# Two graph layers on one core: the steps behind each chunk move from VectorE to GpSimd, Exp to ScalarE, the first loads of adj to SyncE

## The reference, cut to what matters

```python
h = jnp.maximum(_layernorm(x, axis=-1), 0.0)          # x (4096, 128)
# layer 1, in the ball model; adj (4096, 4096)
h = proj(mobius_matvec(weight, h)); h = proj(mobius_add(h, hyp_bias)); x_tangent = logmap0(h)
support_t = adj @ x_tangent
h = proj(expmap0(support_t)); xt = relu(logmap0(h)); x = x + proj(expmap0(xt))
# layer 2: attention over the edges of adj
h = jnp.maximum(_layernorm(x, axis=-1), 0.0)
in_fts = context @ W_common.T                          # context (4096, 256)
logits = (in_fts @ w_left + b_left)[:, None] + (in_fts @ w_right + b_right)[None, :]
logits = where(logits >= 0, logits, 0.2 * logits); logits = where(adj <= 0, -inf, logits)
x = x + relu(softmax(logits, axis=-1) @ h)
```

## Time and profile before

| what | us |
|---|---|
| median of 3 runs | 655.37 (650.78 to 664.92) |
| the profiled execution | 653.83 |
| its span in the trace | 652.0 |
| busy DVE, PE, ACT, POOL | 543.6, 509.1, 422.5, 227.4 |

### The profile page before, as it was taken

One profiled execution on the slowest core, in us unless ns is written; L12 is line 12 of the kernel. 1 busy time (PEld: TensorE's weight loads), 2 busy tenths in 40 slices (PEclk: granted clock), 3 DMA queues, 4 the chain that ended last, 5 costly groups with the idle time before them and its releaser, 6 DMA issues.

```text
span 652.0 us, 9315 instructions
## 1 busy us (share of the span) xinstructions
PE 509.1 (78%) x2695; PEld 318.2 (49%) x2695; DVE 543.6 (83%) x1057; ACT 422.5 (65%) x553; POOL 227.4 (35%) x217
## 2 busy tenths in 40 slices
PE   0360899758768948899898575779898989999995
PEld 0350343223223313344242254568787878787874
DVE  3488797959779836697777899999999999999995
ACT  0584785535345533567474987488888897989881
POOL 4370017984966706910101567420202020202110
PEclk9995799979969968899999888799999999999999
DMA  8991599969969999999999101001110101011010
GB/s 198 273 191 32 106 244 284 259 150 231 237 120 245 142 198 268 238 252 296 252 288 249 35 2 32 14 21 35 24 41 18 33 16 32 16 32 32 0 32 16
DMA packets 164235, 84.51 MB, mean 130 GB/s; under 512 B 7248, under 2 KB 163152, under 8 KB 164208
## 3 DMA queue, kind: packets, MB, share of 16 engines
q1 hardware_dynamic: 93760, 49.30, 35.2%
q10 hardware_dynamic: 70192, 34.74, 25.9%
q0 software_dynamic: 256, 0.15, 0.1%
HBM read 79.96 MB, written 4.21 MB: 129 GB/s over the span
## 4 chain that ended last, share of the span: by engine, by line
DVE 41%; PE 15%; issue 13%; POOL 11%; DMA 10%; SPq 4%; ACTq 3%; ACT 2%; DVEq 1%; POOLq 0%
PE ps L620 11%; DMA room<-in_adj_dram 8%; DVE room L1091 6%; DVE room L1137 5%; DVE mask L1091 5%; POOL mask L458 4%; DVE room L1147 4%; DVE mask L1137 3%; PE ps L646 3%; DVE room L905 3%; POOL mask L453 3%; DVE mask L1147 3%; SPq L331 2%; DMA out_dram<-xk 2%; ACTq L664 2%
## 5 line engine op out<-in xcount | busy, mean ns | idle before, releaser
L620 PE MATMUL ps<-room 128*128 128x512 f32 x512 | 248.7, 636 | 66.7 <-DVE room L905 45.8
L772 ACT ACTIVATE mask<-room 128x1024 int8<-128x1024 f32 x128 | 134.8, 1054 | 124.1 <-DVE room L905 111.3
L905 DVE STREAM_TRANSPOSE room<-room 128x512 f32<-128x512 f32 x256 | 171.4, 694 | 48.3 <-DMA room<-in_adj_dram 16.9
L620 PEld LDWEIGHTS ps<-room 128*128 128x128 f32 x512 | 98.1, 201 | 211.8 <-DVE room L905 109.9
L646 PE MATMUL ps<-room 128*128 128x258 f16 x1152 | 141.8, 285 | 28.5 <-DVE room L1147 28.5
L646 PEld LDWEIGHTS ps<-room 128*128 128x128 bf16 x1152 | 115.2, 101 | 53.9 <-DVE room L1147 34.3
L646 PE MATMUL ps<-room,mask 128*128 128x258 f16 x896 | 101.2, 273 | 9.5 <-DVE h_room L1161 6.4
L646 PEld LDWEIGHTS ps<-room,mask 128*128 128x128 bf16 x896 | 86.3, 97 | 23.1 <-DVE h_room L1161 8.1
L818 ACT ACTIVATE room<-mask 128x2048 bf16 (+1 forms) x36 | 68.5, 1903 | 14.1 <-PE ps L646 14.0
L555 POOL TENSOR_TENSOR h_room<-h_room 128x512 f32<-128x512 f32 x7 | 9.9, 1408 | 146.5 <-DVE post L1172 146.5
L818 ACT ACTIVATE mask<-mask 128x2048 bf16 (+1 forms) x28 | 53.3, 1903 | 4.7 <-PE ps L646 4.7
(11 more groups left out here) (164 smaller groups left out, 551.5 us busy)
## 6 DMA issues: line engine op xcount, KB each, us to landing
room<-in_adj_dram SPq DMA_DIRECT2D x128, 256.0 KB, 8.9
room<-in_adj_dram ACTq DMA_DIRECT2D x128, 256.0 KB, 8.3
mask<-in_L_gnn_context_dram SPq DMA_DIRECT2D x16, 256.0 KB, 11.2
xk<-in_x_dram SPq DMA_DIRECT2D x32, 64.0 KB, 6.4
out_dram<-xk SPq DMA_DIRECT2D x32, 64.0 KB, 5.8
h_room<-out_dram SPq DMA_DIRECT2D x32, 64.0 KB, 2.5
out_dram<-h_room SPq DMA_DIRECT2D x28, 64.0 KB, 1.8
mask<-in_x_dram SPq DMA_DIRECT2D x8, 128.0 KB, 6.6
```

The source lines that it names most:

```text
L620: pe.matmul(acc[parity], xt[:, k, :], turned[:, k % TSLOTS, :], start=(k == 0), stop=(k == NK - 1)).then_inc(block_multiplied, 1)
L772: nc.scalar.activation(mc[:, half * HB:(half + 1) * HB, :], turned[:, slots:slots + HB, :], ACT.Sign).then_inc(half_signed, 1)
L905: v.transpose(turned[:, k % TSLOTS, :].rearrange("p (l b i) -> p b l i", l=L, b=NQ), loaded[:, g % XSLOTS, :, l * Q:(l + 1) * Q].rearrange ...
```

## The change

Of the post work, VectorE keeps relu, the two sums, statistics and variance. GpSimd takes shrink, the coefficient and the residual (now two steps over 128 by 512 elements: relu_u times coefficient, and that plus xk), and affine. What was one piece of the list (a product and its sums) is now two, and one piece stands behind each of shrink, residual and affine. Statistics and variance stand behind steps 28 to 30 instead of 23 to 25. The largest right value is a maximum on VectorE over r_col, a store of 128 elements to DRAM, a load of them into all partitions and a second maximum; both transfers are issued by GpSimd. The four factors are one Exp on ScalarE in chunk 7; GpSimd scales two of them. ScalarE's tanh moves to half 9 and normed of chunk p to half 2 of the chunk after the next. SyncE stores x1 behind tile 4 and loads x behind tile 6. SyncE issues all four quarters of the first four tiles of adj; ScalarE issues the first part of x ahead of weight and bias. Some scratch tiles (the left and right values, the products) get other places, and the loops over the chunks of phase 1 are written out on VectorE and GpSimd.

```diff
...
+                    first_tiles = isinstance(c, int) and c == 0 and g < XSLOTS
+                    for b in (0, 2, 1, 3) if first_tiles else LOW:
                         sp.dma_start(loaded[b * Q:(b + 1) * Q, g % XSLOTS], rows[g, b]).then_inc(
                             adj_in[g % XSLOTS], 16)
                     if isinstance(c, int) and c == 0 and g == XSLOTS - 1:
                         load_nodes(cx, cx_l, cx_in, range(NQ))
-                    if g == 1 and not (isinstance(c, int) and c < 2):
+                    if g == 4 and not (isinstance(c, int) and c < 2):
                         store_x1(c - 2)
-                    if g == 3 and not (isinstance(c, int) and c < 1):
+                    if g == 6 and not (isinstance(c, int) and c < 1):
...
+            def store_largest():
+                pool.wait_ge(top_ready, 1)
+                pool.dma_start(top_dram, extreme[:, 0:1]).then_inc(top_stored, 16)
+            def everyones_largest():
+                pool.wait_ge(top_stored, 16)
+                pool.dma_start(top_row, top_dram.rearrange("p a -> a p").broadcast_to([P, P])).then_inc(top_loaded, 16)
             def exponents():
-                R = extreme[:, 2:3].broadcast_to([P, NK])
+                pool.wait_ge(top_ready, 2)
+                R = extreme[:, 1:2].broadcast_to([P, NK])
                 pool.wait_ge(nl_stored, 16)
...
+                tt(a_col, a_col, lr[:, 0, :], ALU.subtract).then_inc(exponents_ready, 1)
+                tt(b_col, b_col, lr[:, 0, :], ALU.subtract).then_inc(exponents_ready, 1)
+            def scaled_weights():
+                pool.wait_ge(exponentials_done, 1)
+                two = factors[:, 2:4, :].rearrange("p a k -> p (a k)")
+                tt(two, two, constants[:, 1:2].broadcast_to([P, 2 * NK]), ALU.mult).then_inc(factors_ready, 1)
+            part_order = [last_part] + list(range(last_part))
+            turns = [(w, part) for part in part_order for w in range(2)]
+            def beside(n):
+                w, part = turns[n // 2] if n < 2 * len(turns) else (None, None)
+                if part is not None:
+                    product_of(w, part) if n % 2 == 0 else sum_of(w, part)
+                elif n == 2 * len(turns):
+                    sums_and_rows()
+                elif n == 2 * len(turns) + 1:
+                    store_largest()
+                elif n == 2 * len(turns) + 2:
+                    everyones_largest()
+                elif n == 2 * len(turns) + 3:
+                    exponents()
+            def shrink(p):
+                UI, RN, F, VN = (post[:, a:a + L] for a in (8, 12, 20, 24))
+                pool.wait_ge(sums_ready, p + 1)
+                chain = Steps(pool, post_step, p * POOL_POST)
+                chain(tt(post[:, 8:16], post[:, 0:8], powers[:], ALU.pow))
+                chain(nc.gpsimd.tensor_scalar(F, UI, ARTANH_RIM, 1.0, ALU.mult, ALU.min))
+                tt(VN, F, RN, ALU.mult).then_inc(shrunk_ready, 1)
+                chain(tt(post[:, 16:20], post[:, 4:8], powers[:, 0:L], ALU.pow))
+            def residual(p):
+                INV, TH_, TF, CO = (post[:, a:a + L] for a in (16, 28, 32, 56))
+                pool.wait_ge(tanh_ready, p + 1)
+                chain = Steps(pool, post_step, p * POOL_POST + 3)
+                chain(nc.gpsimd.tensor_scalar(TF, TH_, MAX_NORM, None, ALU.min))
+                chain(tt(CO, TF, INV, ALU.mult))
+                chain(tt(relu_u[:], relu_u[:], CO.unsqueeze(2).broadcast_to([P, L, D]), ALU.mult))
+                pool.wait_ge(xk_loaded, p * (16 * NQ) + 16 * NQ)
+                tt(xk[:], relu_u[:], xk[:], ALU.add).then_inc(x1_ready, 1)
+            def affine(p):
+                pool.wait_ge(var_ready, p + 1)
+                chain = Steps(pool, post_step, p * POOL_POST + 6)
+                nc.gpsimd.tensor_scalar(post[:, 44:48], mv[:, :, 0], -1.0, None, ALU.mult)
+                chain(tt(post[:, 48:52], post[:, 40:44], powers[:, 0:L], ALU.pow))
+                tt(post[:, 36:40], post[:, 44:48], post[:, 48:52], ALU.mult).then_inc(norm2_ready, 1)
+            POOL_POST = 7
...
+            beside(0)
+            beside(1)
+            for p in range(NC - 1):
+                shrink(p)
+                beside(3 * p + 2)
+                if p == NC - 2:
+                    scaled_weights()
+                residual(p)
+                beside(3 * p + 3)
+                affine(p)
+                beside(3 * p + 4)
...
-                    norms(NC - 1)
+                    shrink(NC - 1)
+                if g == 2:
+                    residual(NC - 1)
                 if g == 4:
-                    inverse_std(NC - 1)
+                    affine(NC - 1)
...
+            def load_x_high(l):
+                for b in HIGH:
+                    act.dma_start(by_l(x_in, l)[b * Q:(b + 1) * Q], x_l[l, b]).then_inc(x_in_sem[l], 16)
+            load_x_high(0)
             act.dma_start(W_in, weight).then_inc(weights_in, 16)
             act.dma_start(b_colv, bias.rearrange("(d a) -> d a", a=1)).then_inc(weights_in, 16)
             act.dma_start(bias_b, bias.rearrange("(a d) -> a d", a=1).broadcast_to([P, D])).then_inc(weights_in, 16)
                 for b in HIGH:
                     act.dma_start(loaded[b * Q:(b + 1) * Q, g % XSLOTS], rows[g, b]).then_inc(adj_in[g % XSLOTS], 16)
-            for l in range(L):
-                for b in HIGH:
-                    act.dma_start(by_l(x_in, l)[b * Q:(b + 1) * Q], x_l[l, b]).then_inc(x_in_sem[l], 16)
-            for g in range(XSLOTS):
-                load_high(adj_n[0], g)
+            for l in range(1, L):
+                load_x_high(l)
...
-                return {0: copy, 4: squares, 8: tanh, 15: normed}
+                return copy, squares, tanh, normed
             acc_of = [None]
             def signs(c, parity):
                 number = isinstance(c, int)
                 acc_of[0] = acc[1 - parity]
-                steps = {} if number and c == 0 else post_steps(c - 1)
+                steps = {}
+                if c >= 1:
+                    copy, squares, tanh, _ = post_steps(c - 1)
+                    steps = {0: copy, 4: squares, 9: tanh}
+                if c >= 2:
+                    steps[2] = post_steps(c - 2)[3]
+                if c == NC - 1:
+                    steps[7] = exponentials
...
+            def exponentials():
+                act.wait_ge(exponents_ready, 2)
+                every = factors[:].rearrange("p a k -> p (a k)")
+                nc.scalar.activation(every, every, ACT.Exp).then_inc(exponentials_done, 1)
             for c in range(NC):
                 signs(c, c % 2)
             acc_of[0] = acc[1]
-            last = post_steps(NC - 1)
-            last[0]()
+            last_copy, last_squares, last_tanh, last_normed = post_steps(NC - 1)
+            last_copy()
+            post_steps(NC - 2)[3]()
...
+                    if not first:
+                        dve.wait_ge(x1_ready, p)
...
-                def shrink():
-                    dve.wait_ge(norms_ready, p + 1)
-                    chain(v.tensor_scalar(F, UI, ARTANH_RIM, 1.0, ALU.mult, ALU.min))
-                    v.tensor_tensor(VN, F, RN, ALU.mult).then_inc(shrunk_ready, 1)
-                def coefficient():
-                    dve.wait_ge(tanh_ready, p + 1)
-                    v.reciprocal(INV, VN)
-                    chain(v.scalar_tensor_tensor(out=TF, in0=TH_, scalar=MAX_NORM, in1=F, op0=ALU.min, op1=ALU.mult))
-                    chain(v.tensor_tensor(CO, TF, INV, ALU.mult))
-                def residual(ls):
-                    if ls[0] == 0:
-                        dve.wait_ge(xk_loaded, p * (16 * NQ) + 16 * NQ)
-                    for l in ls:
-                        ins = v.scalar_tensor_tensor(out=xk[:, l, :], in0=relu_u[:, l, :], scalar=CO[:, l:l + 1],
-                                                     in1=xk[:, l, :], op0=ALU.mult, op1=ALU.add)
-                    if ls[-1] == L - 1:
-                        ins.then_inc(x1_ready, 1)
...
-                def affine():
-                    dve.wait_ge(std_ready, p + 1)
-                    if not first:
-                        dve.wait_ge(h2_ready, p)
-                    v.scalar_tensor_tensor(out=post[:, 36:40], in0=mv[:, :, 0], scalar=-1.0, in1=post[:, 48:52],
-                                           op0=ALU.mult, op1=ALU.mult).then_inc(norm2_ready, 1)
-                return {7: relu, 12: sums_u, 13: sums_relu, 17: shrink, 20: coefficient,
-                        21: lambda: residual((0, 1)), 22: lambda: residual((2, 3)), 23: lambda: spread((0, 1)),
-                        24: lambda: spread((2, 3)), 25: variance, 29: affine}
+                return {7: relu, 12: sums_u, 13: sums_relu, 28: lambda: spread((0, 1)), 29: lambda: spread((2, 3)),
+                        30: variance}
...
+                    if c == NC - 2 and k == 15:
+                        dve.wait_ge(r_ready, 1)
```

(40 more changed lines are left out.)

82 lines of the change are left out of this document (36 added, 46 removed).

## The result

The changed kernel takes 648.5 us (median of 20 runs, 638.1 to 653.0) beside 653.8 for the kernel before on the same chips: a gain of 5.3 us where 35 were forecast. The profiled execution took 651.0 (span 648.7), 2.5 above its median.

What follows compares the result with a forecast made beforehand. The DMA engines were taken to bound the undisturbed chunks, with stalls added elsewhere: 653.8 - 8.4 (preparation) - 23.9 (chunks) - 2.9 (attention) = 618.6, given as 619 us; forecast range 608 to 631, wider range 606 to 641.

Steps and rivals of the forecast that it cites:

- the price of a chunk: Chunks 1 to 7 of adj: 8.91 MB each at 269 GB/s, 33.1 us, a gain of 23.9 us in all.
- the head: Preparation: ACT's first relu starts earlier as SyncE issues the first four tiles; gain 8.4 us, bounds 0 and 9.9.
- Stage C: Attention, from 363 us to the end: chunk 7's post steps leave DVE's chain; -2.9 us (0 to -6.7).
- a full ring: Chunks: all four adj tile buffers filled during a DVE stall, given as why 144 to 164 us ran only 231 GB/s.
- Rival (2): Chunks: DMA engines give less, 231 GB/s, 38.6 us a chunk, no gain there; 642 us, or 636 at 250 GB/s; chance 0.11.
- The second cost: Preparation: SyncE issues 16 loads instead of 8 before context; costed at nothing, about 8 us if uncovered.
- The price of the shared port: Chunks: GpSimd instructions holding DVE on their common port; about 1 us of stall, inside 5 us slack, costed at nothing.
- rival (1): Chunks: the GpSimd and DVE port remains the loss, variance and residual late, some 22 us back; 641 us, chance 0.09.
- rival (5): Chunks: x loaded late, DVE stops at statistics, 10 us in each of six chunks; slower, 679 us, chance 0.04.
- The round trip: Chunks 6 to 7: largest right value stored to DRAM and loaded back, 7 us each way, hidden, cost 0.
- The table: Chunk 7: the Exp on ACT needs between none and two table loads of 1.28 us, in idle time.
- The hole of neg_left: Transposing store of 4096 four-byte pieces, moved to the start of chunk 6, still costs the adj stream 11.1 us.

Runs made afterwards that it cites:

- with the values turned: The changed kernel with the negated left values transposed on DVE, then stored in 128-byte instead of four-byte pieces; 629.6 us, 0.962.

## Why the prediction was wrong

**The step that failed** is the price of a chunk: "at 269 GB/s that is 33.1 us", and with it "7 x 33.1 + 11.1 = 242.8". The chunks took 270.9 us. The stalls went as forecast, but a chunk without stalls ran at 229 GB/s where it was given 269, 39.5 and 38.6 us in chunks 4 and 5. Against the forecast, chunks 1 to 5 are 184.4 - 165.5 = 18.9 us over, chunk 6 is 51.8 - 44.2 = 7.6 over, chunk 7 1.5 over. That is 28.0 of the 32.4 us between the sum of 618.6 and the profiled 651.0; the head fell short by 1.6 and Stage C by 2.2, and the last 0.6 is rounding and time outside the span.

**The reason given for 269 was untested.** The trace of before held 231 GB/s and 269 at one share, and the prediction laid that to a full ring. A full ring is not the cause: the kernel after is starved (98.8 us of waiting for adj) and slow, and the kernel with x on GpSimd is fast while its ring is often full (SyncE waited 71.3 us for DVE to free tiles, 11.8 in the kernel after). Rates of 287 and 290 GB/s at shares of 1.21 and 1.20, in 15 to 20 and 20 to 25 us of the kernel before, had been read too and were left out; a third rate at one share would have said that a cause was missing. Rival (2) was the true one, "no gain in the chunks", 642 us; it had 0.11. The prediction's own sign of being wrong, "starved stretches below 260 GB/s", is what the trace shows, 233.

**What sets the rate** was shown by five kernels that differ in the quarters and sources alone, with x on GpSimd's queue: both halves of the partitions written at once, about 289 GB/s in the first chunks (three kernels, 631 to 633 us); one half, 226 to 230, with near sources or far ones (two kernels, 670 and 674 us), though the two queues are served equally. One queue alone, whose transfers follow each other, gives 223. With this the kernel after reads so: it is fast while SyncE's and ScalarE's loads get equal service and slow when the engines serve one queue in bursts, for a burst writes one half. That reading rests on the packets counted above (249 GB/s against 219), and on the kernel with x on GpSimd, where 154 of 247 half microseconds are evenly split and move 281 GB/s; no run forced bursts upon a kernel. The Trainium skill, page SBUF — State Buffer, section "Door 1: The DMA port swizzle", has partitions 0 to 63 and 64 to 127 on different ports, with which this agrees. Its section "Can I just issue two DMAs to hit both halves?" says no, since two at once gained only 6% there; here 289 GB/s with two queues on the two halves, against 223 with one queue and 226 with two on one half, says yes, for transfers of 256 KB in 512-byte pieces, and the measurement decides. No run here tried one transfer over all 128 partitions.

**What upsets the interleaving** is settled only in part. Taking x1 and x out of SyncE's queue, with the bytes still moved, gave 18.2 us in the chunks, and spare stores without waits cost far less rate. That leaves SyncE's waits at them and the loads of x among those of adj, and no run changed either alone. The waits are a weak candidate: in 138 to 264 us SyncE waited 3.9 us for x1's landing in the kernel after, and 3.8 with the values turned, yet the rates there were 233 and 249 GB/s. Why a queue keeps the engines for a microsecond or two stays open, as does the decay in chunks 4 and 5 when no x moves at all.

**The head**, -8.4: the relu came 7.2 us earlier and chunk 1 6.8. Right, and short by the x block that the bound had named; in the times it is the whole gain, 0.986 alone. The second cost, "if it were uncovered it would be one queue's slower issue", is partly real: SyncE alone loads at 214 GB/s in 18 to 26 us where both queues had moved 291, and that stays hidden.

**The post work on GpSimd.** The price of the shared port in the chunks was right: no step of a few elements on DVE took over 0.31 us, and rival (1) had no part. x came late, 33 us of waiting on GpSimd in all, as rival (5) had it, but never so late that DVE waited for what follows from it. Waits of DVE in 96 to 362 us (us in total, times, longest):

```profile
DVE room L972 <- DMA room<-in_adj_dram: 97.9, 43, 10.5
DVE room L972 <- ACT mask L830: 4.8, 6, 1.5
DVE room L972 <- PE ps L670: 2.3, 2, 1.7
```

GpSimd is not among them. The late x stands in a group of the page, the transfers in the DMA issues of the trace:

```profile
L552 POOL TENSOR_TENSOR xk<-relu_u,xk 128x512 f32<-128x512 f32 x8 | 10.2, 1278 | 33.3 <-DMA xk<-in_x_dram 33.2
...
xk<-in_x_dram SPq DMA_DIRECT2D x32, 64.0 KB, 7.4
...
neg_left<-h_room POOLq DMA_DIRECT2D x1, 16.0 KB, 20.1
top_right<-h_room POOLq DMA_DIRECT2D x1, 0.5 KB, 11.9
```

**The round trip** was costed at nothing, and DVE reads it at 328.07 without a wait. Its store took 11.9 us, not 7, and its load 7.9 (the DMA issues list it as h_room from top_right); the margin was wide enough. The table: Exp brought no further table load in the chunks (one of 1.28 us there, as before).

**The hole of neg_left** was 11.1; chunk 6 took 51.8 - 38.6 = 13.2 us more than its neighbour, and 282 to 290 us moved 53 GB/s at a share of 1.36. Mechanism right, size 2 us off. **Stage C** was -2.9, measured -0.7; the steps left DVE there, and the time behind the last transpose hardly changed. This was not followed further. One reading was wrong without a term that rests on it: "635 ns mean, 75.7 / 172 = 440 ns" sets the length of a record beside busy time per record, and records overlap; the mean record of that same stretch is 605 ns, and in 96 to 362 us it is 627 in the kernel after.

## What to carry to other kernels

When the DMA share stands at its ceiling, read the GB/s beside it in every stretch, the preparation too, and the duration of a packet: two rates at one share are a cause still to be found, and the lower one is the price until it is. A stall that is removed beneath a transfer limit gives only what the limit leaves, so test the limit before the stall. For loads in 512-byte pieces, let two queues write the two halves of the partitions at the same time and give small transfers a third, as was the fastest here; and do not store single elements across partitions beside them.

## What the runs showed of the hardware that was not expected

- A 512-byte packet takes 33.5 ns when both halves of the partitions are written at once and about 44 ns when one is, at a DMA share of 1.19 and 1.21: 289 GB/s against 226. Same queues, same engines, same bytes; only the partitions written in step differ.
- Two queues with work outstanding are not always served in turn: 174 packets of one to 27 of the other in half a microsecond, reversed 2 us later, with transfers of both under way.
- 4096 pieces of four bytes cost the adj stream some 13 us beside it (chunk 6), 10 of which came back by turning 128 x 32 values on DVE first.
